# Moving six of ScalarE's eight checks of the adjacency codes within a graph: three to later steps of layer 0, three to the border between the layers

## What is computed

```python
# layer 0 (adj is 0 or 1 here; e_of(a) = leaky(einsum('bid,bjd->bij', h * a, h)))
alpha = jnp.where(adj == 1, e0, neg_inf)     # adj == 2, 3, 4 pick e1, e2, e3
out0 = jnp.einsum('bij,bjd->bid', sigmoid(alpha), h) + bias
x = layernorm(x + out0)
# layer 1
Hh = x @ W;  s = Hh @ a_src;  d = Hh @ a_dst
e = jnp.where(adj != 0, jnp.exp(-leaky_relu(s[:, None] + d[None, :])), 0)
x = layernorm(x + elu((e @ Hh) / rowsum(e)))
```

## Time and profile before

| | |
|---|---|
| median of 3 runs | 1369.13 us (1368.9 to 1372.04) |
| the profiled execution | 1369.6 us, of which its span 1367.8 us, 1.8 us around it |
| TensorE's granted clock, mean | 0.993 of full speed |
| PE busy | 1275.9 us, 93% of the span |
| DVE busy | 1029.2 us, 75% |
| ACT busy | 856.0 us, 63% |
| POOL busy | 842.4 us, 62% |
| a graph takes | 82.6 us, nearly the same in all |

### The profile page before, as it was taken

The page is one execution under the profiler, slowest core; times in us unless marked ns, Lnnn a source line. Parts: engine busy times, 40 slices in busy tenths (PEclk is TensorE's granted clock), DMA queues, the critical chain, the costliest instruction groups (busy, mean ns, idle before and its releaser), DMA issues.

```text
span 1367.8 us, 27395 instructions
## 1 busy us (share of the span) xinstructions
PE 1275.9 (93%) x7874; PEld 1139.3 (83%) x7874; DVE 1029.2 (75%) x2594; ACT 856.0 (63%) x2130; POOL 842.4 (62%) x1228
## 2 busy tenths in 40 slices
PE   5799999999999999999999999999999998999986
PEld 4788888888888888888888888888888888888875
DVE  5777778787777877778777787877878777787865
ACT  4746757476575756757476575756757567574643
POOL 4746749476583855839466583865839567394732
PEclk9999999999999999999999999999999999999999
DMA  8162350614325162350624415153250623406001
GB/s 173 32 109 74 67 109 19 119 58 87 94 41 102 45 111 73 59 113 12 121 63 73 104 28 110 54 100 80 54 119 16 111 73 65 108 14 124 28 5 34
DMA packets 190352, 101.73 MB, mean 74 GB/s; under 512 B 140656, under 2 KB 173808, under 8 KB 190320
## 3 DMA queue, kind: packets, MB, share of 16 engines
q1 hardware_dynamic: 171888, 67.79, 21.2%
q0 software_dynamic: 18432, 33.56, 14.6%
HBM read 84.55 MB, written 16.78 MB: 74 GB/s over the span
## 4 chain that ended last, share of the span: by engine, by line
PE 39%; POOL 24%; DVE 20%; issue 11%; ACT 5%; DMA 0%; DVEq 0%; POOLq 0%; ACTq 0%
POOL coef_lo L369 13%; PE acc_bank L1227 11%; PE hh_bank L1206 5%; DVE coef L880 5%; PE acc_bank L1108 4%; PE acc_bank L1110 4%; PE acc_bank L1109 4%; PE lg_bank L1108 3%; PE lg_bank L1110 3%; PE lg_bank L1109 3%; POOL var_eps L377 3%; POOL rstd L380 2%; POOL rstd L390 2%; DVE stats L920 2%; DVE reluP L915 2%
## 5 line engine op out<-in xcount | busy, mean ns | idle before, releaser
L1227 PE MATMUL acc_bank<-H,coef 128*128 128x258 f32 x2048 | 469.1, 382 | 10.9 <-ACT reluP L606 9.6
L1227 PEld LDWEIGHTS acc_bank<-H,coef 128*128 128x128 f32 x2048 | 381.7, 190 | 73.7 <-issue 20.2
L369 POOL TENSOR_TENSOR coef_lo<-coef,coef_hi 128x1024 fp32r<-128x1024 f32 x128 | 305.7, 2389 | 62.2 <-ACT coef_hi L552 60.3
L1108 PE MATMUL acc_bank<-h_hi,coef_hi 128*128 128x256 f32 x1024 | 297.4, 290 | 0.0
L1110 PE MATMUL acc_bank<-h_hi,coef_lo 128*128 128x256 f32 x1024 | 286.3, 280 | 0.0
L1109 PE MATMUL acc_bank<-h_lo,coef_hi 128*128 128x256 f32 x1024 | 286.1, 279 | 0.0
L880 DVE SCALAR_TENSOR_TENSOR coef<-tr_bank,E_col,codeT 128x256 f32<-128x256 f32 x512 | 209.1, 476 | 39.3 <-PE acc_bank L1227 36.8
L1108 PEld LDWEIGHTS acc_bank<-h_hi,coef_hi 128*128 128x128 f32 x1024 | 194.8, 190 | 1.0
L1109 PEld LDWEIGHTS acc_bank<-h_lo,coef_hi 128*128 128x128 f32 x1024 | 195.0, 190 | 0.0
L1110 PEld LDWEIGHTS acc_bank<-h_hi,coef_lo 128*128 128x128 f32 x1024 | 194.7, 190 | 0.0
L552 ACT ACTIVATE coef_hi<-coef 128x1024 fp32r<-128x1024 f32 x128 | 135.7, 1060 | 84.6 <-DVE coef L819 84.1
(11 more groups left out here) (77 smaller groups left out, 2283.5 us busy)
## 6 DMA issues: line engine op xcount, KB each, us to landing
code_nat<-in_adj POOLq DMA_DIRECT2D x128, 256.0 KB, 5.3
x_raw<-in_x SPq DMA_DIRECT2D x16, 1024.0 KB, 5.6
out<-x SPq DMA_DIRECT2D x128, 128.0 KB, 1.7
codeT<-code_nat SPq DMA_TRANSPOSE x128, 3.3
W_ext<-in_L_gnn_W SPq DMA_DIRECT2D x1, 256.0 KB, 4.2
eluE<-in_L_gnn_a SPq DMA_DIRECT2D x1, 256.0 KB, 4.6
bias_bc<-in_L_gnn_bias SPq DMA_DIRECT2D x1, 128.0 KB, 4.1
a_col<-in_L_gnn_a SPq DMA_DIRECT2D x4, 1.0 KB, 4.6
```

Of the source, the lines that this page charges most:

```text
L369: nc.gpsimd.tensor_tensor(coef_lo[:, t % 4, :, :], blocks(coef[:, t % 4, :]), f32(coef_hi[:, t % 4, :, :]), ALU.subtract).then_inc(S.lo0, 1)
L1108: nc.tensor.matmul(dst, lhs_hi, rhs_hi, start=first, stop=False)
L1227: ins = nc.tensor.matmul(acc_bank[t % 2][:, 0:HC], coef[:, SLOT1[t], J * P:(J + 1) * P], H[:, J, :], start=J == 0, stop=J == NT - 1)
```

## The change

The checks of tiles 0 and 1 stay in steps 0 and 1. The checks of tiles 2, 3 and 4 go to steps 5, 6 and 7, at the end of the step, so that steps 2, 3 and 4 have none. The checks of tiles 5, 6 and 7 go to the border: behind the scaling of chunk 4 and ahead of `keep_H` of tile 7, behind the scaling of chunk 5, and behind the scaling of chunk 6. The number of instructions of every kind that compute is the same; no other engine's list changes.

```diff
-                    if t < 6:
+                    if t < 2:
                         watch_codes(b, t)
                     if 1 <= t and t + 3 < NT:
                         high0(F, b, t + 3, prev)
...
                     if nxt and 6 <= t:
                         scale_scores(b + 1, t - 6)
-                    if t in (6, 7):
-                        watch_codes(b, t)
+                    if 5 <= t < 8:
+                        watch_codes(b, t - 3)
...
                 if nxt:
                     scale_scores(b + 1, 4)
+                watch_codes(b, 5)
                 keep_H(F, b, 7, prev, False)
                 ends_H(F, b)
                 if nxt:
                     scale_scores(b + 1, 5)
+                watch_codes(b, 6)
                 if nxt:
                     scale_scores(b + 1, 6)
+                watch_codes(b, 7)
```

## The result

| | before | after |
|---|---|---|
| median of 12 runs each | 1369.02 us (1368.29 to 1373.86) | 1372.17 us (1370.62 to 1373.88) |
| the profiled execution's span | 1367.8 us | 1370.9 us |
| mean granted clock | 0.993 | 0.993 |

The changed kernel takes 1.0019 of the time before, with a 95% interval of 1.001 to 1.0028: 3.15 us more, where 2.2 more were forecast. The interval leaves out no change, and the difference is under the 0.3% that the prediction set as its bound.

A forecast was written before the change was run, and what follows sets the result against it. PE, busy 93% of the span, was taken to set the pace, so only its waits could be won back. A border cost of 0.61 less a gain of 0.46, in 15 graphs, gave +2.2: about 1371.4 us, range 1364 to 1378.5.

The forecast's parts named there:

- The wait for tile 1: Steps 2 to 4: PE's wait of 1.50 us for `x1` of tile 1 stays unchanged, gain 0.
- The check in step 2: Without it ACT's `coef_hi` of tile 5 starts 0.80 us sooner; PE's 0.67 us wait for `x1` of tile 2 goes.
- The part given back in tile 3: PE's wait of 0.56 us for `x1` of tile 3 grows by 0.21, as `var_eps` comes only 0.46 sooner.
- signs of being wrong: Listed beforehand: PE waiting for `x1T` or `H` in steps 6, 7; DVE for the last check; other `coef_lo` or mask lengths.
- The sum of the gain: Steps 2 to 4 together gain 0.46 us a graph, at the least 0.28, at the most 0.67.
- Steps 5 to 7: ACT's idle 1.59 us before `scale_col` of tile 4 covers the moved check, 0.46 left; cost 0, other end 0.1.
- The border: A check holds `scale_col` of tile 7 0.61 us later (0.5 to 0.7); PE's wait there grows from 0.38 to about 1.0.
- The sum: Border cost less gain, 0.61 - 0.46 = +0.15 us in each of 15 graphs: +2.2 us.
- The first: Rival: POOL's root is second to the mask of tile 6; gain only 0.28 a graph, 1374.1 us, slower; chance 0.33.
- The second: Rival: border costs less or steps 2 to 4 give more; 1366.6, or 1359.8 us if tile 3's wait goes; chance 0.17.
- the third: Rival: moved checks only change places, slack making up border cost and gain; within 1 us of 1369.1; chance 0.08.

The follow-up runs named there:

- e3: Kernel before, with only step 2 freed: checks of tiles 2 to 7 stand one step later, in steps 3 to 8, none at the border; 1362.55 us.
- e1: Changed kernel, with the check of tile 5 moved from the border to step 8, behind the scaling of chunk 2; 1364.31 us.
- e2: Kernel before, checks 0 to 4 unmoved, 5 and 6 in steps 6 and 7, 7 at the border ahead of `keep_H` of tile 7; 1380.18 us.
- p0: Kernel before, with POOL's `coef_lo` of tiles 4 to 7 one step later, behind the root instead of ahead of the next; 1431.71 us.
- p1: e1 with POOL's `coef_lo` of tiles 4 to 7 one step later, behind the root, as in p0; 1432.19 us.
- e4_two_checks_at_border: Changed kernel, with the checks of tiles 5 and 6 both ahead of `keep_H` of tile 7; 1398.08 us.

## Why the prediction was right, point by point

**The wait for tile 1: 0.** It is 1.59 where it was 1.50 in the graph shown, and 1.50 to 1.60 before and 1.56 to 1.59 after in nearly all graphs. Right.

**The check in step 2.** `coef_hi` of tile 5 was to start 0.12 behind the mask and did so 0.11 behind it; `coef_lo` was to end before the mask of tile 6 begins (638.11 against 638.55) and the mask to take 1.13; it took 1.15. `norm0` of tile 2 was to be 0.74 sooner and was 0.71. PE's wait of 0.67 is gone. e3 shows that this one check is the whole gain.

**The part given back in tile 3.** The wait was to grow by 0.21 and grew by 0.25, and `var_eps` stands behind `coef_lo` as worked out. One of the signs of being wrong did show: the mask of tile 7 took 1.55 and not the 1.29 of before. The prediction had not worked out that this mask, now sooner, would meet `coef_lo` of tile 6. It cost nothing: the mask ends at 644.52, and `norm0` waits for POOL's root until 644.96.

**The sum of the gain: the term that was a little large.** 0.46 was forecast, 0.40 measured by e1. The step is the choice of the graph: between its first and third wait PE took 10.52 us there, in most other graphs of the loop before 10.41 to 10.46, as the wait for tile 2 was 0.58 to 0.71 by graph and 0.67 in this one. In the changed kernel it is 10.04 to 10.06 in all but two, which take 10.41 and 10.42 with a lower granted clock (a mean of 0.63 from 552 to 556 us in the one and of 0.66 from 1134 to 1138 us in the other). From the usual 10.43 to the usual 10.04 it is 0.39.

**Steps 5 to 7: nothing.** ACT has 0.48 left before `scale_col` of tile 4, where 0.46 was forecast, and PE has no new wait for `x1T` or `H`.

```profile
654.78 0.17 ACT L574 ACTIVATE scale_col<-hh_bank 128x1 f32<-128x1 f32 x1 [0.48 <-PE hh_bank L1209]
```

**The border.** 0.61 was forecast, 0.64 is the row and the measured cost in e2. PE's wait is 1.01 where about 1.0 was forecast. The 0.03 come from `scale_col` starting 1.14 behind the check's start instead of 1.13 and the check starting 1.26 behind the scalings' where I took 1.24.

**The sum.** 15 x (0.64 - 0.40) = 3.6, against 3.1 in the spans and 3.15 in the medians; forecast were 2.2. The two misses, 0.06 and 0.03 a graph, have the same sign, so the sum wasn't saved by errors that cancel.

**The rivals.** The first was half right in its mechanism and wrong in its price: POOL's `rstd` of tile 2 was indeed second to the mask and took 1.06 us instead of 0.75, but it ended at 639.64, before the mask's end at 639.70, so it cost nothing; `var_eps` had slipped in ahead of the mask as the prediction argued. The second and the third fall by e1 and e2. The exclusion of DVE by POOL, which the prediction read from the mask of tile 5, is what decided p0 later.

## To carry to other kernels

An off-path engine's filler work belongs where the engine waits for somebody else, and not ahead of an instruction that a third engine waits for: the same check of 1.13 us cost 0.40, 0.64 or nothing by its place. A gain and a loss of like size hide in a result near zero; move one piece at a time, and keep the half that gains. When a chain crosses several engines, look for the long instruction that stands in the order ahead of a short one on the path, and when it is moved make sure that it doesn't start just before a short instruction that it shuts out: here an idle 0.6 us ahead of the long one took 73 us off p1. When PE waits more, look at the granted clock as well: in p0 over a third of the loss was PE's busy time and not its waits.

## What the runs showed of the hardware

- DVE's `tensor_scalar` over 128x256 from and to SBUF took 0.41 us alone and 2.43 when POOL's `coef_lo` had begun 0.06 us before it; 0.81 when POOL's addition of the bias (0.72) had. It ends 0.14 to 0.15 us behind POOL's instruction each time.
- POOL as the second: `rstd` took 0.55 with no such mask beside it, 1.06 when it began 0.03 us behind the start of DVE's mask of 1.15; it ended 0.06 before the mask did.
- A wait that stands on a register instruction ahead of the instruction proper costs 0.11 to 0.12 us from the releaser's end instead of 0.03: `coef_hi` of tile 6 starts 0.03 behind the mask in the kernel before, where the wait is on the rounding itself, and 0.12 behind it in the changed one.
- A check on ACT holds up the next instruction for 1.13 us, but the next check for 1.27 (the kernel before) to 1.33 (e4_two_checks_at_border), as that waits for the first one's semaphore.
- Behind waits of PE of 1 to 1.6 us the granted clock stayed at 1.00 in most graphs, but in a few it fell to 1.2 GHz for a while (a mean of 0.79 over 8 us in e4_two_checks_at_border, whose two such graphs took 1.8 and 2.0 us more than the others). In p0_root_first, with most of the waits for `x1` at 1.6 to 2.4 us and 82.1 us of them in all, it fell often enough for a mean of 0.978 over the span, and the aggregation's matmuls came 0.21 us apart instead of 0.12 while it was down. Why in some graphs and not in the rest stays open.
